# A four-layer graph network on one Trainium2 core: its layers on two scaled 16-bit floats a value, with the count matrix read in place

## The chip, the cores and the metric

The kernel runs on one core of one Trainium2 chip. The metric is the device time in microseconds (us), shown as the median of several executions. Everything is one launch.

## The reference

There are 2048 nodes with 512 features and 67,584 edges: 32,768 random pairs, their reverses and one loop a node, sorted by destination. Four blocks follow one another, each as x = x + block(relu(layernorm(x))):

```python
# block 0: attention inside each of 32 graphs of 64 nodes, 8 heads, a bias per edge added to the scores
attn = einsum(q, k) * scale; attn[b, src, dst] += edge_attr @ We + be; out = softmax(attn) @ v @ Wo + bo
# block 1: three GCN layers; deg counts the in-edges plus the loop, dis = rsqrt(deg)
h = segment_sum((h @ W)[row] * dis[row] * dis[col], col) + b        # relu after the first and the second
# block 2: one GCN layer with the degrees counted at the source, bias inside, relu outside
out = relu(segment_sum(dis[row] * dis[col] * (x @ W.T + b)[row], col))
# block 3: a sum with one weight an edge
out = relu(segment_sum((features @ W)[src' ] * edge_weight, dst'))
```

So five products (2048x512 by 512x512) are each followed by a sum over neighbours. The kernel does the sums of blocks 1 and 2 as products with a dense matrix of edge counts (2048x2048), and the last as a product with a dense matrix of summed edge weights.

## The kernel before, in words

It has four stages, one after another. **Edge prep** (`edge_prep`, to 68 us) counts edges, computes the edge biases, the degrees (`keep.dis1`, one reciprocal root a node) and the statistics of the first layer norm. **Build** (`build_matrices`, to about 497 us) takes the edges in 64 batches. In each, VectorE (DVE) makes one-hot matrices, TensorE (PE) multiplies them (L875 for the attention bias, L880 for counts and weights), ScalarE (ACT) copies counts and the first part of the weights out of PSUM, and DVE adds the second part into `w_slab` (L651). PE transposes the slab four batches later (L826), and it goes to DRAM as f32. The projections q, k and v are spread over the same batches (L853, L860). **Attention** ends at 665 us. The rest are the **layers** (`graph_layers`).

The engines are programmed one by one; each runs its own list in order and waits on semaphores. `keep.count` holds the counts as f16, `[partition, source tile, destination]`, with the destinations in an order of class (node within its graph) and then graph. A value of the layers is held as two fp32r parts: `hi` is the value cast (ACT), and `lo` is the value less `hi` (DVE).

- `products(layer)`: for each of 16 tiles, `split_hi` (ACT, L1430) and `split_lo` (DVE, L1669) write two parts of the transposed input, PE runs 12 matmuls of 512 columns (hi.hi, hi.lo, lo.hi over 4 blocks; L1573), and `product_hi` (ACT, L1445) and `product_lo` (DVE, L1682) put the scaled result into `m.g` as two parts. There are two PSUM banks for it. In the fourth layer DVE first adds the bias (L1676).
- `sums(layer)`, for the first four layers: four groups `c` of 512 destinations, 16 steps `i` in each, 8 matmuls a step (L1607) into four banks. Ahead of each step `copy_chunk` (DVE, L1692) rewrites 128x512 counts from f16 to fp32r in natural node order. At the end of a group DVE's `finish` reads the four banks (L1713 in layers 0 and 1), and PE's first step of the next group waits bank by bank for it. In layer 0, DVE also sums the count rows (`sum_out`, L1742), which the fourth layer's degrees need.
- The last layer's sum is 32 steps of 24 matmuls (L1645) on the f32 weight matrix. Each 128x1024 piece is split into parts by ACT (L1536) and DVE (L1767); the result is taken by DVE with relu and x added (L1794).

Layers are numbered 0 to 4 in the code. SyncE (SP) issues loads and stores in one fixed list. Weights share the buffer `m.tiles` with the tiles of x, or `h_t` for the first.

Of the kernel before, what the change touches and what calls it, by code (L numbers as in the profile page):

```python
# [22 lines left out]
NGRAPH = N // GN  # L23

# [17 lines left out]
LN_EPS = 1e-5  # L42

# [18 lines left out]
def prep_memory(nc, mem, keep, m):  # L62
# [24 lines left out]
    m.x_all = keep.count[:].rearrange("p t n -> p (t n)").bitcast(F32)[:, 0:NT * D].rearrange("p (t d) -> p t d", d=D)  # L87
# [21 lines left out]
    m.chosen = small[:, 9 * GN:10 * GN]  # L109
    m.graph_of = small[0:NGRAPH, 11 * GN:11 * GN + 2 * P].rearrange("p (z n) -> p z n", z=2)  # L110
# [4 lines left out]
             "most most_row most_one most_all mask graph_of starts_mm padded var std pool dve "  # L115
# [26 lines left out]
def prep_pool(nc, io, keep, m, s):  # L142
# [38 lines left out]
    pool.wait_ge(s["mask"], 1)  # L181
    for half in range(2):
# [15 lines left out]
def prep_act(nc, io, keep, m, s):  # L198
# [15 lines left out]
    act.sqrt(keep.dis1[:], keep.dis1[:])  # L214
    act.wait_ge(s["var"], 1)
# [3 lines left out]
def prep_pe(nc, io, keep, m, s):  # L219
# [74 lines left out]
    pe.matmul(m.most_ps, m.most_one.to_broadcast([2, P]), keep.ident[0:2, 0:2], start=True, stop=True).then_inc(s["most_all"], 1)  # L294


def prep_dve(nc, io, keep, m, s):
# [74 lines left out]
    op.then_inc(s["graph_of"], 1)  # L372
    dve.wait_ge(s["viol_row"], 1)
# [34 lines left out]
    dve.tensor_scalar(keep.dis1[:], m.deg_ps, 1.0, 1.0, ALU.add, ALU.max).then_inc(s["deg"], 1)  # L408
# [21 lines left out]
    dve.reciprocal(keep.dis1[:], keep.dis1[:])  # L430
    settle(dve.reciprocal(keep.rstd[:], keep.rstd[:]))
# [26 lines left out]
def build_memory(nc, mem, keep, m):  # L458
# [13 lines left out]
    m.w_slab = sb("w_slab", [P, 2, NT, P], F32)  # L472
# [93 lines left out]
def build_dve(nc, io, keep, m, s, first_round):  # L566
# [62 lines left out]
    def evacuate(n):  # L629
# [59 lines left out]
def build_act(nc, io, keep, m, s, first_round):  # L689
# [36 lines left out]
    def copy_sums(n):  # L726
# [72 lines left out]
def build_pe(nc, io, keep, m, s, first_round):  # L799
# [18 lines left out]
    def turn_weights(c):  # L818
# [339 lines left out]
def attention_dve(nc, io, keep, m, s, order):  # L1158
# [3 lines left out]
    for t in range(NT):  # L1162
        diag = keep.count[:, t].rearrange("p (v g) -> p g v", g=NGRAPH)[:, 2 * t:2 * t + 2]
# [57 lines left out]
    dve.tensor_scalar(keep.rstd[:], m.moments[:, :, 1], LN_EPS, None, ALU.add).then_inc(s["var"], 1)  # L1221
# [654 lines left out]
```

## Time and profile before

| | us |
|---|---|
| median of 3 runs | 1617.23 |
| lowest, highest | 1615.29, 1624.25 |
| the profiled execution's own time | 1615.48 |
| its span, first to last instruction | 1614.2 |
| PE busy | 1449.1 |
| DVE busy | 998.7 |
| ACT busy | 529.0 |
| mean granted PE clock, share of full speed | 0.958 |

"Busy" is the union of an engine's instructions. Matmuls are pipelined, so the time of one is longer than the pace at which they follow one another; the pace comes from a burst's length and count. The name `a<-b,c` of a matmul gives output, moving operand, stationary operand. `PEld` is PE's load of the stationary operand. Idle time in square brackets stands ahead of an instruction, with what ended it.

### The profile page before, as it was taken

The page shows a single profiled execution, that of the slowest core. Times are in us where ns is not written, and L with a number is a line of the kernel's source. Part 1 is how long each engine was busy: PE and PEld are TensorE (multiplying, and loading weights), DVE is VectorE, ACT ScalarE, POOL GpSimd, SP SyncE. Part 2 cuts the span into 40 slices and gives each one's busy share as a digit, 9 for nine tenths or more (in the row PEclk, how much of TensorE's full clock was granted, in tenths as well). Part 3 has the DMA queues.
Part 4 walks back from the last instruction along what each step waited for, and adds up shares of the span by engine and source line. Part 5 has one row for each costly group of instructions (what it writes and reads, how often), then busy time and mean ns, then how long its engine had stood idle before and what let it go on. Part 6 is the DMA issues. An engine that isn't in the chain of part 4 may idle for free.

```text
span 1614.2 us, 22068 instructions
## 1 busy us (share of the span) xinstructions
PE 1449.1 (90%) x8875; PEld 1183.5 (73%) x8875; DVE 998.7 (62%) x1487; ACT 529.0 (33%) x994; POOL 96.6 (6%) x74
## 2 busy tenths in 40 slices
PE   7389998999983778499999999999989999799999
PEld 6378887878772444378887888787867777678887
DVE  8789999899996665135884544455546544432322
ACT  1255666545542332462103210321124122432121
POOL 3010010101002300000000000011110000000000
PEclk9689999999996999799999999999999999899999
DMA  7423333344227332320000000002110221642301
GB/s 268 139 68 135 123 117 110 115 143 137 94 94 268 117 112 79 105 78 27 0 1 1 26 1 0 1 26 79 59 52 27 66 66 53 234 168 94 104 1 53
DMA packets 70111, 138.89 MB, mean 86 GB/s; under 512 B 9713, under 2 KB 22129, under 8 KB 68466
## 3 DMA queue, kind: packets, MB, share of 16 engines
q1 hardware_dynamic: 67362, 126.25, 22.5%
q0 software_dynamic: 1280, 5.77, 1.3%
q10 hardware_dynamic: 1360, 5.38, 0.9%
q8 instruction: 73, 1.20, 0.3%
q14 instruction: 36, 0.29, 0.1%
HBM read 84.06 MB, written 53.31 MB: 85 GB/s over the span
## 4 chain that ended last, share of the span: by engine, by line
PE 54%; DVE 2%; ACT 1%; DMA 1%; issue 1%; SPq 0%; DVEq 0%; ACTq 0%
PE banks L1607 29%; PE banks L1573 13%; PE banks L1645 11%; PE banks L1550 1%; DMA h_gcn_t<-in_L_gnn_W 0%; PE banks L1621 0%; DVE tiles L1721 0%; DVE split L1669 0%; DVE g L1682 0%; DMA b_row<-in_L_gnn_b 0%; ACT h_gcn_t L1497 0%; ACT g L1445 0%; DVE tiles L1794 0%; ACT h_gcn L1401 0%; ACT split L1430 0%
## 5 line engine op out<-in xcount | busy, mean ns | idle before, releaser
L1692 DVE CAST split<-count 128x512 fp32r<-128x512 f16 x256 | 162.8, 648 | 192.8 <-PE banks L1607 192.8
L1607 PE MATMUL banks<-g,split 128*128 128x512 f32 x1024 | 244.6, 395 | 0.7 <-DVE tiles L1721 0.6
L1573 PE MATMUL banks<-split 128*128 128x512 f32 x960 | 231.7, 401 | 12.9 <-DVE split L1669 12.6
L1607 PE MATMUL banks<-split,g 128*128 128x512 f32 x1024 | 233.9, 390 | 0.0
L1573 PEld LDWEIGHTS banks<-split 128*128 128x128 f32 x960 | 183.4, 193 | 56.9 <-DVE split L1669 18.5
L1607 PEld LDWEIGHTS banks<-split,g 128*128 128x128 f32 x1024 | 191.2, 188 | 42.4 <-DVE h_gcn_t L1713 3.2
L1607 PEld LDWEIGHTS banks<-g,split 128*128 128x128 f32 x1024 | 188.0, 188 | 45.9 <-DVE tiles L1717 2.8
L1645 PE MATMUL banks<-g,split 128*128 128x512 f32 x768 | 176.0, 392 | 2.9 <-DVE split L1767 2.9
L1645 PEld LDWEIGHTS banks<-g,split 128*128 128x128 f32 x768 | 145.2, 189 | 33.7 <-DVE split L1767 3.3
L627 DVE TENSOR_TENSOR x_sb<-eb_parts,x_sb 128x4096 f16<-128x4096 f16 x64 | 146.5, 2289 | 0.0
L875 PE MATMUL bias_ps<-x_sb 128*128 128x256 f16 x1024 | 125.0, 276 | 17.5 <-DVE bias L637 15.4
L875 PEld LDWEIGHTS bias_ps<-x_sb 128*128 128x128 f16 x1024 | 100.1, 99 | 41.8 <-DVE x_sb L627 16.4
L1767 DVE TENSOR_TENSOR split<-count,split 128x1024 fp32r<-128x1024 f32 x32 | 39.0, 1225 | 119.1 <-ACT split L1536 119.1
L1682 DVE SCALAR_TENSOR_TENSOR g<-banks,dis,g 128x512 fp32r<-128x512 f32 x64 | 48.0, 750 | 75.2 <-ACT g L1445 74.7
L1669 DVE TENSOR_TENSOR split<-h_gcn_t,split 128x512 fp32r<-128x512 f32 x80 | 54.7, 685 | 51.4 <-ACT split L1430 51.4
L1149 PE MATMUL wo_ps<-wo_sb,att_t 128*128 128x512 f32 x128 | 67.3, 674 | 19.9 <-ACT att_t L1082 19.9
L616 DVE TENSOR_TENSOR x_sb<-iota_src,keys 128x2048 f16<-128x2048 f16 x64 | 78.3, 1223 | 0.0
L1445 ACT ACTIVATE g<-banks,dis 128x512 fp32r<-128x512 f32 x64 | 44.1, 689 | 97.3 <-PE banks L1573 68.1
L1536 ACT CAST split<-count 128x1024 fp32r<-128x1024 f32 x32 | 33.3, 1048 | 129.8 <-PE banks L1645 129.8
L1497 ACT ACTIVATE h_gcn_t<-h_gcn_t,b_col 128x512 f32<-128x512 f32 x32 | 20.5, 712 | 161.2 <-DVE h_gcn_t L1713 161.2
L651 DVE SCALAR_TENSOR_TENSOR w_slab<-cw_ps,w_first 128x512 f32<-128x512 f32 x64 | 67.5, 1054 | 8.9 <-ACT w_first L737 8.8
L1430 ACT CAST split<-h_gcn_t 128x512 fp32r<-128x512 f32 x80 | 49.2, 617 | 47.5 <-PE banks L1607 47.5
(212 smaller groups left out, 1811.3 us busy)
## 6 DMA issues: line engine op xcount, KB each, us to landing
weight_dram<-w_new SPq DMA_DIRECT2D x64, 256.0 KB, 2.4
count<-weight_dram SPq DMA_DIRECT2D x32, 512.0 KB, 6.7
tiles<-x_dram SPq DMA_DIRECT2D x48, 256.0 KB, 2.6
qk_dram<-stage SPq DMA_DIRECT2D x64, 128.0 KB, 1.9
qk<-qk_dram SPq DMA_DIRECT2D x8, 1024.0 KB, 6.9
x_dram<-tiles SPq DMA_DIRECT2D x32, 256.0 KB, 2.2
count<-in_x SPq DMA_DIRECT2D x4, 1024.0 KB, 11.8
h<-in_x SPq DMA_DIRECT2D x16, 256.0 KB, 3.7
```

Of the source, the lines that this page charges most:

```text
L616: dve.tensor_tensor(m.hot_src[:, z].rearrange("p g (c two) -> p g c two", two=2), keep.iota_src[:].rearrange("p (c two) -> p c two", two=2 ...
L627: dve.tensor_tensor(m.hot_eb[:, z].rearrange("p g (t c) -> p g t c", t=NT), values, tiles, ALU.mult).then_inc(s["hots"], 1)
L651: dve.scalar_tensor_tensor(slab, m.cw_ps[:, :, 2 * CCOLS:CW].rearrange("p b (h s) -> p b h s", h=2), 1.0 / LOW, m.w_first[:].rearrange("p ...
L875: mm = pe.matmul(m.bias_ps[:, 0:NT * HP], m.hot_src[:, z, g], m.hot_eb[:, z, g], start=g == 0, stop=g == BATCH - 1)
L1149: mm = pe.matmul(m.wo_ps[:, t % 2], m.att_t[:, k, :], m.wo[:, k, :], start=k == 0, stop=k == KT - 1)
L1430: act.copy(m.h_parts[:, t % 2, 0], m.h_t[:, :, t * P:(t + 1) * P]).then_inc(s["hi"], 1)
L1573: mm = pe.matmul(m.prod_ps[:, slot], m.h_parts[:, slot, zh, k], m.w_parts[:, zw, k], start=n == 0, stop=n == len(passes) - 1)
L1607: mm = pe.matmul(m.agg_ps[:, b], lhs, rhs, start=i == 0 and z == 0, stop=i == NT - 1 and z == 1)
L1645: mm = pe.matmul(m.banks[:, b], m.part[:, n % 3, z, b * P:(b + 1) * P], m.g[:, q, gz], start=q == 0 and (z, gz) == (0, 0), stop=q == NT - ...
L1669: dve.tensor_tensor(m.h_parts[:, t % 2, 1], m.h_t[:, :, t * P:(t + 1) * P], m.h_parts[:, t % 2, 0].bitcast(F32), ALU.subtract).then_inc(s[ ...
L1682: dve.scalar_tensor_tensor(lo, result, dis[:, t:t + 1], hi.bitcast(F32), ALU.mult, ALU.subtract).then_inc(s["glo"], 1)
L1692: dve.tensor_copy(m.chunk[:, n % 4].rearrange("p (g v) -> p g v", v=GN), keep.count[:, i].rearrange("p (v g) -> p g v", g=NGRAPH)[:, graph ...
```

## The change

- Everything in the layers that was fp32r becomes f16 in two parts, with power-of-two scales. Each weight matrix, each group of 512 columns of h in layers 1 and 2, and the edge weights get a scale from their largest absolute value. The maximum is reduced along the free dimension on DVE, moved to one row by a PE transpose (`peak_row`), turned into an exponent in a row of small DVE operations on one partition, and sent to all partitions by a small matmul (`peak_all`).
- The counts are f16 operands in place: `copy_chunk`, `m.chunk` and its 256 copies go. `keep.count` is now `[P, NT, GROUPS, GN, GPC]`, that is by chunk of 512 destinations, class and the 8 graphs of the chunk. So the sums come out in that order: `finish` of layers 0 and 1 writes back to natural order, x is loaded and stored in that order by DMA (`x_own`), the fourth layer's split reads `h_t` through a strided view, and a second set of degrees (`odis1`, `odis2`) is made in that order, with new work in edge prep and in layer 1.
- `w_slab` is written in the order of the sums, and the PE transposes read it with a stride.
- `sum_out` takes a maximum of each count row besides the sum, and all 16 tiles are done at four a group, ahead of `finish`.
- Layers 1 and 2 use three PSUM banks for products, and `product_hi`/`product_lo` run one tile later. Weights have a buffer of their own; three pieces of the edge weights are loaded early; relu after the last sum moves from DVE to ACT.

```diff
-    m.g = sb("g", [P, NT, 2, D], F32R)
-    m.split = sb("split", [P, 3, KT * D], F32R)
+    m.g = sb("g", [P, NT, 2, D], F16)
+    m.h_parts = sb("h_parts", [P, 2, 2, KT, P], F16)
+    m.w_parts = sb("w_parts2", [P, 2, KT, D], F16)
+    m.part = sb("part", [P, 3, 2, HALF], F16)
...
-        slab = m.w_slab[:, q % 2].rearrange("p s (c b h) -> p c b h s", c=4, h=2)[:, n % 4]
-        dve.scalar_tensor_tensor(slab, m.cw_ps[:, :, 2 * CCOLS:CW].rearrange("p b (h s) -> p b h s", h=2), 1.0 / LOW,
-                                 m.w_first[:].rearrange("p b (h s) -> p b h s", h=2), ALU.mult, ALU.add).then_inc(s["slab"], 1)
+        slab = m.w_slab[:, q % 2, n % 4].rearrange("p (b c) -> p b c", b=BATCH)
+        dve.scalar_tensor_tensor(slab, m.cw_ps[:, :, 2 * CCOLS:CW], 1.0 / LOW, m.w_first[:], ALU.mult, ALU.add).then_inc(s["slab"], 1)
...
+        tiles = m.w_slab[:, q % 2].rearrange("p c (u s) -> p s (c u)", s=NT)
...
# PE, sums
-            pe.wait_ge(s["chunk"], layer * STEPS + n + 1)
-                        lhs, rhs = m.g[:, i, z, block], m.chunk[:, n % 4]
+                            lhs, rhs = m.g[:, i, z, block], m.count[:, i, c]
...
+                if c == 0:
+                    if i == 2:
+                        pe.wait_ge(s["glo"], (layer + 1) * NT)
+                        peak_row()
+                    if i == 4:
+                        peak_all()
...
+                elif layer < 2:
+                    if i == 6:
+                        peak_row()
+                    if i == 8:
+                        peak_all()
...
# PE, products
+            if layer in (1, 2) and t == 2:
+                peak_row()
+            if layer in (1, 2) and t == 3:
+                peak_all()
...
# DVE
+    def exponent():
+        dve.wait_ge(s["peak_row"], peaks + 1)
+        settle(dve.tensor_reduce(m.line[:, 8:9], m.peak_row, axis=AX.X, op=ALU.max))
+        settle(dve.tensor_scalar(m.line_i[:, 0:1], m.line[:, 8:9].bitcast(I32), 23, None, ALU.logical_shift_right))
+        settle(dve.tensor_scalar(m.line_i[:, 0:1], m.line_i[:, 0:1], 16, None, ALU.max))
...
+    def h_scale(layer, c):
+        row = m.h_line[:, layer - 1]
+        for k in range(KT):
+            dve.wait_ge(s["relu_h"], ((layer - 1) * GROUPS + c) * KT + k + 1)
+            op = dve.tensor_reduce(m.h_max[:, k:k + 1], m.h_t[:, k, c * COLS:(c + 1) * COLS], axis=AX.X, op=ALU.max)
+        settle(op)
+        dve.tensor_reduce(m.peak[:, 0:1], m.h_max[:], axis=AX.X, op=ALU.max).then_inc(s["peak"], 1)
+        exponent()
...
+            to_all(op, m.h_scale[:, layer - 1, c:c + 1], 1).then_inc(s["h_scaled"], 1)
...
# DVE, finish of layers 0 and 1
-                dve.tensor_tensor(m.h_t[:, b, cols], m.agg_ps[:, b], m.dis_row[:, cols], ALU.mult).then_inc(s["fin"], 1)
+                out = m.h_t[:, b, c * COLS:(c + 1) * COLS].rearrange("p (g v) -> p v g", g=GPC)
+                pair = [a.rearrange("p (v g) -> p v g", g=GPC) for a in (m.agg_ps[:, b], m.dis_row[:, c * COLS:(c + 1) * COLS])]
+                dve.tensor_tensor(out, *pair, ALU.mult).then_inc(s["fin"], 1)
...
+            if c == GROUPS - 1:
+                split_lo(layer + 1, 2)
+            h_scale(layer + 1, c)
...
     def sum_out(i):
-        dve.tensor_reduce(m.dis2[:, i:i + 1], keep.count[:, i], axis=AX.X, op=ALU.add).then_inc(s["out_sum"], 1)
+        row = m.count[:, i].rearrange("p c n -> p (c n)")
+        dve.tensor_reduce(m.dis2[:, i:i + 1], row, axis=AX.X, op=ALU.add)
+        dve.tensor_reduce(m.count_max[:, i:i + 1], row, axis=AX.X, op=ALU.max).then_inc(s["out_sum"], 1)
...
# DVE, sums
+        for c in range(GROUPS):
+            if c == 0:
+                weight_peak(layer + 1)
+                weight_scale(layer + 1)
+                if layer == 1:
+                    edge_scale()
+                    out_degrees()
+                for k in range(KT):
+                    weight_lo(layer + 1, k)
...
+            if layer == 0:
+                for i in range(PER):
+                    sum_out(c * PER + i)
...
+            finish(layer, c)
...
# the split of the fourth layer reads h_t so
+        cols = m.h_t[:].rearrange("p k (c v g) -> p k c g v", c=GROUPS, g=GPC)[:, :, t // PER, first:first + 2]
```

## Rows read from the trace of the kernel before

**Rows 1.** The page, part 1: busy time by engine over the span.

```profile
PE 1449.1 (90%) x8875; PEld 1183.5 (73%) x8875; DVE 998.7 (62%) x1487; ACT 529.0 (33%) x994; POOL 96.6 (6%) x74
```

**Rows 2.** The chain that ended last, by line (the page, part 4, second line).

```profile
PE banks L1607 29%; PE banks L1573 13%; PE banks L1645 11%; PE banks L1550 1%; DMA h_gcn_t<-in_L_gnn_W 0%; PE banks L1621 0%; DVE tiles L1721 0%; DVE split L1669 0%; DVE g L1682 0%; DMA b_row<-in_L_gnn_b 0%; ACT h_gcn_t L1497 0%; ACT g L1445 0%; DVE tiles L1794 0%; ACT h_gcn L1401 0%; ACT split L1430 0%
```

**Rows 3.** Busy time in stretches: us, PE, PEld, DVE, ACT, POOL, PE clock, DMA.

```profile
200.00:300.00 100.00, 93.47 (x780) 82.01 (x779) 93.51 (x122) 59.05 (x111) 9.59 (x4) 0.98 0.35 118
...
sum 405.00, PE 373.45 PEld 328.21 DVE 382.98 ACT 222.49 POOL 32.74; mean PE 62.24 PEld 54.70 DVE 63.83 ACT 37.08 POOL 5.46
...
740.00:857.00 117.00, 117.00 (x515) 95.75 (x514) 84.03 (x98) 11.29 (x19) 0.00 (x0) 1.00 0.03 10
...
1246.00:1372.00 126.00, 125.27 (x565) 99.98 (x563) 61.29 (x118) 30.07 (x83) 0.00 (x0) 1.00 0.19 59
```

**Rows 4.** The chain in order of time, pieces of the layers.

```profile
665.81 8.03 DMA h_gcn_t<-in_L_gnn_W
...
678.78 4.67 PE banks L1621 x32
...
740.30 116.83 PE banks L1607 x512
...
864.12 38.37 PE banks L1573 x168
...
1434.86 171.23 PE banks L1645 x747
```

**Rows 5.** Engines in order of time, build: start, us, engine, line, count.

```profile
301.13 1.91 PE L875 MATMUL bias_ps<-x_sb 128*128 128x256 f16 x16
...
303.56 0.62 PE L826 MATMUL work_ps<-ident,w_slab 128*128 128x128 f32 x4
...
208.67 1.14 PE L815 MATMUL work_ps<-ident,gathered 128*128 128x128 f32 x8
```

**Rows 6.** Groups of instructions by line and form, 120 to 560 us.

```profile
L651 DVE SCALAR_TENSOR_TENSOR w_slab<-cw_ps,w_first 128x512 f32<-128x512 f32 x59 | 62.2, 1054 | 7.1 <-ACT w_first L737 6.9
...
L595 DVE SCALAR_TENSOR_TENSOR fields<-fields,scale,eb_parts 128x1024 f32<-128x1024 f32 x7 | 14.5, 2068 | 0.0
...
L716 ACT ACTIVATE eb_parts<-fields 128x1024 f16<-128x1024 f32 x7 | 13.8, 1973 | 0.0
```

**Rows 7.** The same view, 665 to 1614 us.

```profile
L1767 DVE TENSOR_TENSOR split<-count,split 128x1024 fp32r<-128x1024 f32 x32 | 39.0, 1225 | 119.1 <-ACT split L1536 119.1
...
L1536 ACT CAST split<-count 128x1024 fp32r<-128x1024 f32 x32 | 33.3, 1048 | 129.8 <-PE banks L1645 129.8
...
L1742 DVE TENSOR_REDUCE dis<-count 128x1 f32<-128x2048 f16 x16 | 36.5, 2279 | 0.0
...
L1713 DVE TENSOR_TENSOR h_gcn_t<-banks,dis_row 128x512 f32<-128x512 f32 x32 | 19.8, 678 | 0.0
...
L1669 DVE TENSOR_TENSOR split<-h_gcn_t,split 128x512 fp32r<-128x512 f32 x80 | 54.7, 685 | 51.4 <-ACT split L1430 51.4
...
L1692 DVE CAST split<-count 128x512 fp32r<-128x512 f16 x256 | 162.8, 648 | 192.8 <-PE banks L1607 192.8
```

**Rows 8.** Engines in order of time, at three idle stretches of PE.

```profile
864.12 16.16 PE L1573 MATMUL banks<-split 128*128 128x512 f32 x70 [1.56 <-DVE split L1669]
...
1200.97 5.49 PE L1573 MATMUL banks<-split 128*128 128x512 f32 x12 [5.64 <-DVE split L1669]
...
1434.86 7.34 PE L1645 MATMUL banks<-g,split 128*128 128x512 f32 x24 [2.88 <-DVE split L1767]
```

**Rows 9.** The chain in order of time, products of the fourth layer.

```profile
1238.27 0.71 DVE banks L1676
...
1241.13 3.07 PE banks L1573 x12
```

**Rows 10.** Engines in order of time, two dependent small operations on DVE.

```profile
66.58 0.17 DVE L423 TENSOR_SCALAR small_i<-small 128x2 int32<-128x2 int32 x1
66.78 0.17 DVE L424 TENSOR_SCALAR small_i<-small_i 128x2 int32<-128x2 int32 x1
```

More of the change, by code:

```diff
@@ L1319, in layers_sp @@
         load_x(t, t % PER)
-    sp.wait_ge(s["relued"], NT)
-    load_weights(1)
-    for layer in (2, 3):
+    for n in range(AHEAD):
+        load_raw(n)
+    for layer in (1, 2, 3):
         sp.wait_ge(s["wlo"], KT * layer)
@@ L1438, in product_hi @@
             act.wait_ge(s["agg"], NT * layer)
-        if layer == 4:
-            act.copy(m.g[:, t, 0], m.prod_ps[:, t % 2]).then_inc(s["ghi"], 1)
-        else:
-            dis = m.dis2 if layer == 3 else keep.dis1
-            if layer == 3:
-                act.wait_ge(s["dis2"], 1)
-            act.activation(m.g[:, t, 0], m.prod_ps[:, t % 2], ACT.Copy, scale=dis[:, t:t + 1]).then_inc(s["ghi"], 1)
+        if layer < 3:
+            act.wait_ge(s["g_scaled"], layer + 1)
+        if layer == 3:
+            act.wait_ge(s["odis2"], 1)
+        scale = G_SHIFT[4] if layer == 4 else m.g_scale[:, layer, t:t + 1]
+        act.activation(m.g[:, t, 0], prod_bank(m, layer, t), ACT.Copy, scale=scale).then_inc(s["ghi"], 1)
     def products(layer):
-        for t in range(NT + 1):
+        late = slots(layer) - 1
+        for t in range(NT + late):
             if t < NT:
@@ L1560, in turn_weights, with peak_row, peak_all @@
         for i in range(KT):
-            mm = pe.transpose(m.turn_ps[:, bank, i * P:(i + 1) * P], m.tiles[:, o, i * P:(i + 1) * P], keep.ident[:])
+            mm = pe.transpose(m.turn_ps[:, bank, i * P:(i + 1) * P], m.w_raw[:, o, i * P:(i + 1) * P], keep.ident[:])
         mm.then_inc(s["wturned"], 1)
+    def peak_row():
+        pe.wait_ge(s["peak"], peaks + 1)
+        pe.transpose(m.peak_row, m.peak[:, 0:1], keep.ident[:]).then_inc(s["peak_row"], 1)
+    def peak_all():
+        nonlocal peaks
+        peaks += 1
+        pe.wait_ge(s["peak_one"], peaks)
+        pe.matmul(m.peak_all, m.ones[:], m.line[:, 0:8], start=True, stop=True).then_inc(s["peak_all"], 1)
     def product(layer, t):
@@ L1616, in layers_pe, with turn_own @@
+    def turn_own():
+        pe.wait_ge(s["dis2_t"], 1)
+        for c in range(GROUPS):
+            for z in range(2):
+                mm = pe.matmul(m.own_ps[:, c], m.spread[:, z, c], m.dis2_t[:, z * GN:(z + 1) * GN], start=z == 0, stop=z == 1)
+        mm.then_inc(s["own"], 1)
     turn(0, 0)
     turn(0, 1)
+    peak_row()
+    peak_all()
     for c in range(GROUPS):
@@ L1695, in products @@
+        dve.scalar_tensor_tensor(lo, result, scale, hi, ALU.mult, ALU.subtract).then_inc(s["glo"], 1)
     def products(layer):
[L1696 to L1697 removed]
+        late = slots(layer) - 1
+        for t in range(NT + late):
+            if t < NT and (t >= (3 if layer in (1, 2) else 2) or layer in (0, 4)):
                 split_lo(layer, t)
[L1699 to L1703 removed]
+            if t >= late:
+                product_lo(layer, t - late)
@@ L1768, in layers_dve @@
+    weight_peak(0)
+    weight_scale(0)
     for k in range(KT):
```

524 lines of the change are left out of this document (329 added, 195 removed).

## The prediction

> **What bounds the kernel now.** I read the page first: PE is busy 90% of the span, DVE 62% [rows 1]. Then the chain that ended last, by line: L1607 (sums), L1573 (products) and L1645 (last sum) hold 53% of the span, all PE [rows 2]. In the table of stretches the layers' sums have PE full (117.00 of 117) at clock 1.00, while the build has both PE and DVE above 90% [rows 3]. So the layers are PE's own pace, and the build is a race of two engines. The pace: 512 matmuls in 116.83 us, 168 in 38.37, 747 in 171.23 are 228.2, 228.4 and 229.2 ns [rows 4].
>
> **Matmuls on f16.** Their number stays: 960 products, 2048 in sums, 768 in the last sum. 512 columns of f16 don't occur before. 256 do, each with another stationary operand: 16 in 1.91 us [rows 5]. With the last one's drawn-out end taken off (about 0.28), the pace is 109 ns, 2.3 above 256 columns at 2.4 GHz; 512 columns then take 213.3 + 2.3 = 215.7 ns. Ends: 228.2 (nothing gained) and 213.3. I take 215.7, the nearest row's. That is 12.5 ns a matmul: 512 give 6.4 us, a warm layer of products at most 2.2, and 768 at 229.2 give 10.3.
> The Trainium skill ("TensorE: Matmul & The Clock Gate", Back-to-back issue gap) also states about 131 ns a matmul for a sustained stream of 512 columns with loads. It would take some 320 us more off (3776 x 85 ns). This trace is against it: 109 ns for half the columns. I give it 1%.
>
> **Strides.** Three rows show what strided f32 work costs. L651 writes with a 512 B step and takes 1054 ns where the contiguous L1713 takes 678: 0.72 ns an element. L595 reads one f16 operand at 32 B steps: 2068 against 1225 for L1767, 0.8 an element. L716 (ACT) reads at 512 B steps: 1973 against 1048 for L1536, 0.9 [rows 6, 7]. Against this stands L1692, a plain copy reading f16 at 64 B steps in 648 ns [rows 7]. The change removes one such access and adds others:
> - Slab: L651 falls to about 0.69, so 64 x 0.36 = 23 us of DVE. But PE is busy 373 of the 405 us from 92 to 497, DVE 383 [rows 3]. With DVE at 361 PE leads, and both hand over through single buffers. The gain lies between 6 and 23; I take 14. The slab's strided loads by PE: eight transposes with strided loads take 1.14 us, four contiguous 0.62 [rows 5], so 121 ns against 114, under 2 us in all, within the 14.
> - `finish` in layers 0 and 1 writes at 256 B steps: 1.04 us a bank for 0.68. PE takes a bank's first two matmuls in 0.43, so each group boundary waits some 1.4 us more.
> - The fourth layer's split reads at 32 B steps on ACT (+0.45) and DVE (+0.4).
>
> The Trainium skill ("SBUF — State Buffer", Door 1: The DMA port swizzle) says that accesses landing on a new 16-byte line each pay. L651, L595 and L716 agree, L1692 doesn't. By the rule the two new strided places cost as above; without it they cost nothing.
>
> **Layer 0's sums: DVE becomes the bound.** `sum_out` is now two reductions of 2048 f16 for each of 16 tiles. One takes 2279 ns (2.19 apart) [rows 7]; a group has 8 = 17.5 us, before its `finish`. A group of PE is 128 x 0.2157 = 27.6 us. In the first group DVE does the last `product_lo` (1.5), the weight maximum (2048 f32, 2.2), waits for PE's small matmuls after steps 2 and 4 (to 9.2), splits weights (to 12.2), and sums (to 29.7). The four banks are free at 33.7, and PE's first step of group 1 ends at 34.2 instead of 29.6. Call the end of that step E. Now `h_scale` of the group before stands in DVE's list ahead of the next sums. It waits for `peak_row` after PE's step 6 (E+10.4) and `peak_all` after step 8 (E+13.8), so it ends at E+14.3. Then 17.5 and four banks at about 1 us: E+36.2, where PE alone needs 27.6. PE idles 6.6 us in between. That happens twice, and the third time DVE reaches layer 1's first `split_lo` at E+31.8+0.7.
> After 5.64 us of idle, PE ran 12 matmuls in 5.49 us, after 2.88 us 24 in 7.34, after 1.56 at full pace [rows 8]: 2.7, 1.8 and 0 us extra at the lower clock. Adding 2.7 twice and 1.8 once: 34.2 + 36.2 + 38.9 + 38.9 - 3.7 + 1.8 = 146.3 us until layer 1's first product, against 116.8: **+29.5**. Ends: below, if reductions were hidden, -5 (6.4 less inserted PE work); above, 40 with slower rewarming.
>
> **Change of layer, 0 to 1 and 1 to 2.** Product 3 of the next layer now needs `g_scale`, and this the maximum over group 3: four banks (4.0), relu on ACT, `split_lo(2)` (0.7), four reductions (2.4), `peak_row`, some ten dependent small operations at 0.2 each [rows 10], `peak_all`, then ghi, glo, split (2.2). PE covers it with products 0 to 2 (7.8) and stands still 2.3 + 2.9 us; before, it was 1.56 [rows 8]. Cost 3.4 us plus 2.6 of lower clock: **+6.0** for 1 to 2. For 0 to 1 DVE starts late, and I count **+7.2**. Ends: 0 and 10 each.
>
> **The other terms** (- is a gain):
> - Edge prep: six more DVE operations (0.2 to 0.5 each) in DVE's filled list before the barrier: +1.9. POOL's three new ones lie under its wait for the edge records.
> - Start of layers: first weights are waited for 8.03 us [rows 4]; now they are issued first, but the maximum and exponent (4.5) follow. ACT meanwhile waits for PE's 4.67 us of `dis` rows [rows 4] as before: +1.
> - Products: layer 0 -1 (ACT is nearly full there), 1 and 2 -2 each.
> - Sums of layer 1: -6.4; boundaries +1.4 x 3; `out_degrees` waits for PE's steps 11 and 13, so weights and `finish` are late by 1.2; inserted PE work 2.2: +1.2. Layers 2 and 3: -6.2 and -6.1. The 256 copies L1692 (163 us of DVE) were hidden behind PE and give nothing.
> - Products of layer 3: before, two products ran per 2.86 (end of one to start of the next but one, 1238.27 to 1241.13) + 3.09 [rows 9], 2.97 each. Now 2.86 + 0.84 + 2.94, 3.32 each; 14 of them +4.9. The missing bias load gives 0.4: +4.5. Without stride costs -1.4.
> - Into layer 4: the first piece of edge weights is split ahead of it (+1.7), one copy instead of four (-0.3): +1.4. Products -2.2; the wait of 2.88 before the last sum [rows 8] goes: -2.8. Last sum -10.3. Relu on ACT at the end +0.7.
>
> **Sum**: 1.9 - 14 + 1 - 1 + 29.5 + 7.2 - 2 + 1.2 + 6.0 - 2 - 6.2 + 4.5 - 6.1 + 1.4 - 2.2 - 2.8 - 10.3 + 0.7 = +6.8. On the profiled execution's 1615.5: 1622.3. The median of the runs stands 1.7 above that execution, so **1624 us**.
>
> **Rivals.**
> 1. Strides are free and the build gives 20. Then -6 (layer 3), -11 (eight `finish`), -6 (build): **1601**. For it: L1692. Against: three rows. 0.26.
> 2. Layer 0's sums stay PE-bound, since the reductions run faster than the row: 29 less, **1595**. Against: the maximum is the same operation on the same data, and the list is in order. 0.06.
> 3. Slower: the lower clock after each new stop. I count six stops. If the many short waits (each bank of `finish`, about 1 us) keep PE from the upper level for 24 to 40 matmuls instead of 12, each of six costs 3 to 6 more: **1642**, and it decides from about 20 matmuls on. For it: 24 matmuls were slowed after only 2.88 us [rows 8]. 0.17.
> 4. f16 is no faster than fp32r, because the 15 ns above 213.3 aren't the type's: +47, **1670**. Against: the f16 row. 0.05.
> 5. The 131 ns rule, 0.01.
> The forecast has 0.45; its own range is 1612 to 1636.
>
> About 0.5% (8 us) can be told from no change. Faster: rivals 1, 2, 5: 0.33. The forecast's 0.45 splits into 0.26 same and 0.19 slower; with rivals 3 and 4 slower is 0.41. The range 1597 to 1648 takes in rival 1 and 3.
>
> **What would show it.** The sums' matmuls at 215 to 216 ns; slab writes near 0.69 us; idle PE of 5 to 7 us ahead of groups 2 and 3 of layer 0, released by DVE's `finish`, with 32 reductions of 2.28; two idles of 2 to 3 us at each change of layer; 1.04 us for `finish`; 3.3 us a product in layer 3. It is wrong if layer 0's sums end within 125 us, or if the matmul's pace stays at 228.

## The result, and the profile after

Four runs of the changed kernel have their median at 1629.33 us (1627.98 to 1631.36), four of the kernel before (the three of the table and one more) at 1618.06 (1615.29 to 1624.25): a ratio of 1.0065, 95% interval [1.0034, 1.0097]. The change costs 11 us by the medians; I forecast 1624. The profiled execution took 1629.89 us, its span is 1628.2.

The page, part 1, answers to [rows 1]: PE's busy time fell by 12 us although the span grew by 14.

```profile
PE 1437.2 (88%) x8942; PEld 859.9 (53%) x8942; DVE 933.9 (57%) x1449; ACT 557.0 (34%) x963; POOL 86.3 (5%) x79
```

The chain of waits of the changed kernel, in order of time (start, us, what), answers to [rows 4].

```profile
662.45 5.79 DMA tiles<-x_dram
...
764.60 15.24 PE banks L1718 x56
...
802.44 15.10 PE banks L1718 x56
...
840.15 15.02 PE banks L1718 x56
...
892.91 35.53 PE banks L1681 x156
...
1056.85 4.28 PE banks L1681 x12
...
1099.64 5.18 PE banks L1718 x24
...
1459.76 160.12 PE banks L1784 x741
```

24 matmuls in 5.18 us are 215.8 ns each, 741 in 160.12 are 216.1, where [rows 4] had 228 to 229. But layer 0's sums, one piece of 116.83 us before, are now cut up by stops, stretches in which PE stands idle (the number in brackets, in us):

```profile
764.60 1.93 PE L1718 MATMUL banks<-count,g 128*128 128x512 f16 x4 [3.24 <-DVE h_gcn_t L1926]
...
802.44 1.03 PE L1718 MATMUL banks<-count,g 128*128 128x512 f16 x2 [6.53 <-DVE h_gcn_t L1926]
...
840.15 15.02 PE L1718 MATMUL banks<-count,g 128*128 128x512 f16 x56 [6.54 <-DVE h_gcn_t L1926]
```

After each stop 56 matmuls take 15.0 to 15.2 us (269 ns) instead of 12.1. The granted clock behind it is 0.50, the lower level of 1.2 GHz (columns: us, PE, PE clock, DMA share and GB/s):

```profile
764.60:770.00 5.40, 5.40 (x13) 0.50 0.00 0
```

The stretch of layer 0's sums (columns as in [rows 3]), where before PE was busy 117.00 of 117 us at clock 1.00:

```profile
733.20:877.50 144.30, 121.73 (x526) 51.31 (x523) 99.82 (x104) 14.22 (x19) 0.00 (x0) 0.93 0.02 8
```

VectorE in order of time in the second group of those sums (start, us, engine, line, what, count, idle time before and who ended it):

```profile
763.53 3.68 DVE L1926 TENSOR_TENSOR h_gcn_t<-banks,dis_row 128x512 f32<-128x512 f32 x4
767.06 2.44 DVE L1861 TENSOR_REDUCE h_max<-h_gcn_t 128x1 f32<-128x512 f32 x4
769.53 0.16 DVE L1863 TENSOR_REDUCE peak<-h_max 128x1 f32<-128x4 f32 x1
779.99 0.28 DVE L1806 TENSOR_REDUCE line<-banks 1x1 f32<-1x128 f32 x1 [10.30 <-PE banks L1661]
...
783.75 0.16 DVE L1823 COPY h_scale<-banks 128x1 f32<-128x1 f32 x1 [2.41 <-PE banks L1668]
783.83 2.27 DVE L1955 TENSOR_REDUCE dis<-count 128x1 f32<-128x2048 f16 x1
...
799.18 2.27 DVE L1956 TENSOR_REDUCE count_max<-count 128x1 f32<-128x2048 f16 x1
801.37 3.69 DVE L1926 TENSOR_TENSOR h_gcn_t<-banks,dis_row 128x512 f32<-128x512 f32 x4
```

From one `finish` to the next are 37.8 us, where PE needs 27.6. VectorE stands still for 10.3 + 2.4 us of them, waiting for PE's small matmuls of `peak_row` and `peak_all`, while eight reductions of the counts are queued behind that wait. Then PE, done with its group, stands still for VectorE: the 6.53 us ahead of 802.44, and 6.54 us ahead of 840.15. Each engine waits once for the other.

The groups of instructions answer to [rows 6, 7] (line, engine, what, count | busy us, mean ns | idle before; L685 in the build, L1926 in the layers, L1496 in the products of layer 3 alone):

```profile
L685 DVE SCALAR_TENSOR_TENSOR w_slab<-cw_ps,w_first 128x512 f32<-128x512 f32 x64 | 43.6, 681 | 14.5 <-ACT w_first L770 14.1
...
L1926 DVE TENSOR_TENSOR h_gcn_t<-banks,dis_row 128x512 f32<-128x512 f32 x32 | 29.7, 1044 | 30.9 <-PE banks L1718 30.9
...
L1496 ACT CAST h_parts<-h_gcn_t 128x512 f16<-128x512 f32 x20 | 20.2, 1015 | 0.0
```

The span, cut at events that both traces have. Each length is read between two starts, each trace being one execution; the starts of matmuls that overlap can be read 0.2 us apart, so tenths are not to be leaned on. The forecast's terms are grouped to the same cuts.

| stretch | before | after | forecast | measured |
|---|---|---|---|---|
| edge prep | 67.9 | 72.4 | +1.9 | +4.5 |
| build and attention | 596.4 | 589.0 | -14 | -7.4 |
| into the layers | 24.7 | 23.6 | +1 | -1.1 |
| products, layer 0 | 51.2 | 48.2 | -1 | -3.0 |
| sums, layer 0 | 116.9 | 144.3 | +29.5 | +27.4 |
| change and products, layer 1 | 45.3 | 50.9 | +5.2 | +5.6 |
| sums, layer 1 | 116.9 | 120.6 | +1.2 | +3.8 |
| change and products, layer 2 | 45.1 | 50.6 | +4.0 | +5.5 |
| sums, layer 2 | 125.6 | 119.3 | -6.2 | -6.2 |
| change and products, layer 3 | 57.0 | 61.3 | +4.5 | +4.2 |
| sums, layer 3 | 123.6 | 118.0 | -6.1 | -5.6 |
| into layer 4 | 15.1 | 16.2 | +1.4 | +1.1 |
| products and last sum | 220.3 | 205.4 | -15.3 | -14.9 |
| end | 8.1 | 8.3 | +0.7 | +0.2 |
| sum | 1614.2 | 1628.2 | +6.8 | +14.0 |

### The profile page after: what moved, and what is told of

Same layout as the page of the kernel before. It is cut to its first block, busy times and chain, and to the rows that moved or that the text cites. A ratio compares the mean times of both kernels' runs of the same rounds, so it can differ in the third digit from the quotient of the medians.

```text
span 1628.2 us, 22078 instructions
## 1 busy us (share of the span) xinstructions
PE 1437.2 (88%) x8942; PEld 859.9 (53%) x8942; DVE 933.9 (57%) x1449; ACT 557.0 (34%) x963; POOL 86.3 (5%) x79
## 4 chain that ended last, share of the span: by engine, by line
PE 47%; DVE 8%; ACT 2%; issue 1%; DMA 0%; ACTq 0%; DVEq 0%; SPq 0%
PE banks L1718 24%; PE banks L1681 11%; PE banks L1784 10%; DVE dis L1955 2%; DVE count_max L1956 2%; PE banks L1644 1%; DVE h_parts L1897 1%; DVE h_gcn_t L1926 1%; ACT h_parts L1496 1%; DVE banks L1905 1%; ACT h_gcn L1465 0%; PE banks L1760 0%; DMA tiles<-x_dram 0%; DVE tiles L1930 0%; DVE stats L1942 0%
## 5 line engine op out<-in xcount | busy, mean ns | idle before, releaser
L1681 PE MATMUL banks<-w_parts,h_parts 128*128 128x512 f16 x960 | 225.5, 396 | 31.5 <-DVE h_parts L1897 19.8
L1718 PE MATMUL banks<-count,g 128*128 128x512 f16 x1024 | 235.0, 389 | 20.0 <-DVE h_gcn_t L1926 20.0
L1718 PE MATMUL banks<-g,count 128*128 128x512 f16 x1024 | 229.5, 379 | 1.1 <-DVE tiles L1934 0.9
L1681 PEld LDWEIGHTS banks<-w_parts,h_parts 128*128 128x128 f16 x960 | 95.2, 101 | 156.5 <-DVE h_parts L1897 26.8
L1718 PEld LDWEIGHTS banks<-count,g 128*128 128x128 f16 x1024 | 98.6, 99 | 149.4 <-DVE h_gcn_t L1926 33.9
L1784 PE MATMUL banks<-g,part 128*128 128x512 f16 x768 | 166.1, 379 | 0.1
L1718 PEld LDWEIGHTS banks<-g,count 128*128 128x128 f16 x1024 | 98.5, 98 | 119.6 <-DVE tiles L1934 6.7
L1784 PEld LDWEIGHTS banks<-g,part 128*128 128x128 f16 x768 | 75.1, 98 | 91.0 <-DVE g L1908 0.6
L1908 DVE SCALAR_TENSOR_TENSOR g<-banks,g_scale,g 128x512 f16<-128x512 f32 x64 | 47.9, 748 | 37.8 <-ACT g L1510 37.8
L894 PE MATMUL work_ps<-h_t,wq_sb 128*128 128x256 f32 x256 | 60.3, 384 | 0.0
L894 PE MATMUL work_ps<-h_t,wk_sb 128*128 128x256 f32 x256 | 59.4, 380 | 0.2 <-ACT fields L734 0.2
```

What stands on the lines that cost most here:

```text
L894: mm = pe.matmul(m.work_ps[:, bank, 0:SCOLS], weights[:, k, c * P:(c + 1) * P], m.h_t[:, k, :], start=k == 0, stop=k == KT - 1)
L1681: mm = pe.matmul(prod_bank(m, layer, t), m.h_parts[:, slot, zh, k], m.w_parts[:, zw, k], start=n == 0, stop=n == len(passes) - 1)
L1718: mm = pe.matmul(m.agg_ps[:, b], lhs, rhs, start=i == 0 and z == 0, stop=i == NT - 1 and z == 1)
L1784: mm = pe.matmul(m.banks[:, b], m.part[:, n % 3, z, b * P:(b + 1) * P], m.g[:, q, gz], start=q == 0 and (z, gz) == (0, 0), stop=q == NT - ...
L1908: dve.scalar_tensor_tensor(lo, result, scale, hi, ALU.mult, ALU.subtract).then_inc(s["glo"], 1)
```

## The experiments

The ratios below are to the kernel before, measured beside each run, with a 95% interval. The changed kernel stands at 1.0065 [1.0034, 1.0097], so its time can't be told from a run whose ratio lies within some 0.3% of it. There the profile of the stage decides, and that is one execution. Differences from the changed kernel in us are between medians taken at different times.

**1. The slab alone, on the kernel before.**

```diff
-        slab = m.w_slab[:, q % 2].rearrange("p s (c b h) -> p c b h s", c=4, h=2)[:, n % 4]
...
+        slab = m.w_slab[:, q % 2, n % 4].rearrange("p (b c) -> p b c", b=BATCH)
...
+        tiles = m.w_slab[:, q % 2].rearrange("p c (u s) -> p s (c u)", s=NT)
```

> The kernel before with one part of the change: the slab is written in the order of its sums, and the transposes read it with a step. The stage from the start of the build to the last slab write took 420.5 us before and 413.3 in the changed kernel, with PE busy 93 and 96% of it. Theory A (PE is what the build waits for once the slab write costs 0.68 instead of 1.05 us): the stage takes 412 to 415 us, the kernel is 6 to 8 us faster than before, and PE is busy over 95% of the stage. Theory B (the changed kernel lost part of the slab's gain to its four smaller count additions, or to other memory places): the slab alone gives the 14 us of the forecast or more, the stage takes 407 or less. Theory C (the slab gives nothing, the stage differs by chance): within 1 us of before.

1608.7 us, 0.9933 [0.9907, 0.9959]. From the end of edge prep to the start of the last slab write are 415.3 us: 5.2 less than before, 0.3 above theory A's upper end; B and C are out. The changed kernel has 413.3, so its smaller count additions cost nothing that this stage shows.

**2. The same without the step in the transposes' reads.** The weight matrix comes out in a wrong order, so this run serves for its times alone.

```diff
-        tiles = m.w_slab[:, q % 2].rearrange("p c (u s) -> p s (c u)", s=NT)
+        tiles = m.w_slab[:, q % 2].rearrange("p c (u s) -> p (c u s)", s=NT).rearrange("p (s u) -> p s u", s=NT)
```

> As the run before it, but the transposes read 128 neighbouring elements of the slab instead of every 16th, so the weight matrix comes out in a wrong order; every instruction is there. Strided weight loads took 196 ns in the changed kernel against 141 contiguous ones before. Theory A (PE binds, and the strided loads are part of what PE does): PE's busy time falls by about 3 to 4 us (256 transposes by some 0.014 us, 64 groups), the stage takes 409 to 411 us, 10 us below before. Theory D (the loads are hidden, PE's hand-over with VectorE through single buffers binds): within 1 us of the run with the step.

1608.4 us, 0.9947 [0.9926, 0.9968]: the times don't tell it from run 1. The stage takes 412.4 us, 2.9 less, in one profile each; eight profiles with the changed kernel's build, steps and all, have 411.1 to 413.5, so a difference of this size is near the spread. The transposes themselves are clearer. Their loads (duration ns min/median/max), and the transposes in PE (busy us, mean ns), with the step (run 1):

```profile
L826 PEld LDWEIGHTS work_ps<-ident,w_slab x256: 186/196/210, 115.8 to 487.3; 128*128 128x128 f32 x128
...
L826 PE MATMUL work_ps<-ident,w_slab 128*128 128x128 f32 x256 | 42.9, 292 | 1.5 <-DVE w_slab L651 1.5
```

and without it (run 2):

```profile
L826 PEld LDWEIGHTS work_ps<-ident,w_slab x256: 138/141/145, 116.9 to 485.1; 128*128 128x128 f32 x128
...
L826 PE MATMUL work_ps<-ident,w_slab 128*128 128x128 f32 x256 | 39.3, 278 | 1.5 <-DVE w_slab L651 1.5
```

Busy times from 92 to 484 us, of the kernel before, of run 1 and of run 2:

```profile
sum 392.00, PE 368.34 PEld 323.85 DVE 380.20 ACT 217.81 POOL 32.74; mean PE 92.09 PEld 80.96 DVE 95.05 ACT 54.45 POOL 8.19
```

```profile
sum 392.00, PE 378.26 PEld 333.92 DVE 366.79 ACT 219.07 POOL 28.57; mean PE 94.57 PEld 83.48 DVE 91.70 ACT 54.77 POOL 7.14
```

```profile
sum 392.00, PE 373.95 PEld 329.94 DVE 368.09 ACT 220.25 POOL 28.69; mean PE 93.49 PEld 82.48 DVE 92.02 ACT 55.06 POOL 7.17
```

VectorE was the fuller engine before. With its slab writes cut by 24 us PE is the fuller one (96%), and without the step PE is busy for 4.3 us less, 3.6 of them in the transposes. So the build gains only until PE is in its way. The strided loads cost PE 3.6 us of work; that about 3 of them reach the stage fits the two profiles, but isn't shown by them alone. The Trainium skill ("SBUF — State Buffer", Door 1: The DMA port swizzle) has accesses that land on a new 16-byte line each pay; the loads with a 64 B step agree, 196 against 141 ns.

**3. The maxima of the counts away from layer 0.** The 16 reductions go to layer 1's groups, the edge scale to layer 2's.

```diff
-        dve.tensor_reduce(m.dis2[:, i:i + 1], row, axis=AX.X, op=ALU.add)
-        dve.tensor_reduce(m.count_max[:, i:i + 1], row, axis=AX.X, op=ALU.max).then_inc(s["out_sum"], 1)
+        dve.tensor_reduce(m.dis2[:, i:i + 1], row, axis=AX.X, op=ALU.add).then_inc(s["out_sum"], 1)
...
+            if layer == 1:
+                for i in range(PER):
+                    max_count(c * PER + i)
```

> The changed kernel with the 16 maximum reductions of the counts moved from layer 0's sums to layer 1's (4 in each group, behind the weights), and the edge scale that needs them to layer 2's. Nothing is left out. Per group VectorE then reduces 9.1 us instead of 18.2 in layer 0 and 9.1 instead of 0 in layer 1. Theory A (in layer 0 VectorE's list is the bound, because the reductions stand behind a scale that waits for PE's steps 6 and 8): the group's list ends at E+14.3+9.1 = E+23.4, before PE's 27.6, so layer 0's sums fall from 144.3 to 117 to 119 us, layer 1's stay at 120.6, the kernel takes 1602 to 1606 us. Theory B (the strided finish and the inserted PE work cost layer 0 its time, the reductions only happen to stand there): layer 0's sums stay above 130 us. Theory C (the work only moves the loss): layer 1's sums grow by over 10 us.

1606.2 us, 0.9944 [0.9921, 0.9966]. Layer 0's sums take 116.7 us. The two stretches of the sums in this run, layer 1's and layer 0's (columns as in [rows 3]), and the stop in layer 1's:

```profile
896.40:1026.00 129.60, 117.95 (x542) 52.30 (x541) 69.11 (x97) 14.33 (x20) 4.95 (x4) 0.96 0.06 17
729.50:846.20 116.70, 114.11 (x525) 50.27 (x524) 66.83 (x90) 14.22 (x19) 0.00 (x0) 1.00 0.03 10
...
936.59 3.76 PE L1718 MATMUL banks<-count,g 128*128 128x512 f16 x8 [9.92 <-DVE h_gcn_t L1926]
```

A is shown for layer 0: 27.6 us came from one list. The strided `finish` and the inserted PE work are still there, so B is out. C was half right: layer 1's sums grew by 9.0, since in its first group the reductions stand behind `out_degrees`, which waits for PE's steps 11 and 13, and VectorE reached `finish` only at 935.5. The net gain of the two stretches is 18.6 us. Of the 24 us by which this profile is shorter than the changed kernel's, 3.6 lie ahead of the layers, where the edit touches nothing.

**4. Fixed factors for layers 1 and 2's values.** In place of the measured ones; the groups' reductions, exponents and PE's small matmuls for them are left out.

```diff
-            op = dve.tensor_reduce(m.h_max[:, k:k + 1], m.h_t[:, k, c * COLS:(c + 1) * COLS], axis=AX.X, op=ALU.max)
...
-        exponent()
...
+        if c < GROUPS - 1:
+            dve.memset(m.h_scale[:, layer - 1, c:c + 1], 2.0 ** 12).then_inc(s["h_scaled"], 1)
```

> The changed kernel with fixed factors (2^12) for layers 1 and 2's values instead of measured ones: the eight groups' reductions, the exponents on one partition and PE's two small matmuls for each are left out. Both count reductions stay in layer 0. Theory A (layer 0 loses its time to VectorE's wait for PE's steps 6 and 8 plus the 18.2 us of reductions, and the two changes of layer lose 5 us each to the chain from the last bank to g_scale): with the wait gone a group's list ends at about E+4.3+18.2 = E+22.5, before 27.6, so layer 0's sums fall to 117 to 119 us (-26), the stretches from the end of the sums to the next layer's sums fall from 50.9 and 50.6 to about 45 (-5.5 each), 1591 to 1595 us in all. Theory B (volume of the reductions alone is the bound): layer 0's sums stay above 130. Theory C (the changes of layer lose to the strided finish and the split, not to the scale): they stay at 49 to 51.

1585.1 us, 0.9799 [0.9773, 0.9825]. Layer 0's sums take 120.2 us with all 32 count reductions in place, so volume alone (theory B) is out: either cure works, because the loss needs the wait and the reductions behind it. What is left above run 3 is the first stop, still 3.23 us: in the first group the reductions stand behind the weight's scale, which waits for PE's steps 2 and 4. The changes of layer are read in the chain of this run:

```profile
853.65 41.44 PE banks L1681 x192
895.09 5.18 PE banks L1714 x24
...
1014.28 41.44 PE banks L1681 x192
```

16 products without any stop are 41.4 us, for 50.9 and 50.6 in the changed kernel, so theory C is out. I had expected 45: that was the stretch before, which held its own stop and the slower matmuls. The scale costs 9.5 and 9.2 us, not 5.5.

**5. The fourth layer's reordering on ScalarE's copies.**

```diff
+            out = m.h_t[:].rearrange("p k (c g b v) -> p k c b v g", c=GROUPS, g=GPC, b=PER)[:, :, c, b]
+            for k in range(KT):
+                op = act.copy(out[:, k], source[:, k].rearrange("p (v g) -> p v g", g=GPC))
...
-        cols = m.h_t[:].rearrange("p k (c v g) -> p k c g v", c=GROUPS, g=GPC)[:, :, t // PER, first:first + 2]
```

> The changed kernel with the reordering for the fourth layer done where ScalarE copies the transposed tiles out of PSUM (it writes them in the natural order, four copies of 128x128 instead of one of 128x512), so that the two splits of that layer read neighbouring elements. Nothing is left out. Before it, one product of that layer takes 3.45 us, a chain through two engines: bias addition 0.70, g's high half 0.69, split 1.11 on ScalarE with a step, split 1.07 on VectorE with a step. Theory A (this chain sets the layer, and the step costs what the forecast took, 0.4 to 0.45 on each engine): the period falls to 2.6 to 2.75, where PE takes over, and the products' stretch from 61.3 to about 50 us, -10 us in all (1619). Theory B (the layer is bound elsewhere, the split's step only fills idle time): no more than 2 us. Theory C (the strided write costs ScalarE what the strided reads did, and the last chunk's four copies lie in the chain): -5 us.

1620.4 us, 1.0028 [1.0010, 1.0047]: 9 us below the changed kernel by the medians, 6 by the ratios. The groups of instructions from 720 to 1400 us:

```profile
L1478 ACT COPY h_gcn_t<-banks 128x128 f32<-128x128 f32 x64 | 16.7, 414 | 30.9 <-PE banks L1646 30.9
L1502 ACT CAST h_parts<-h_gcn_t 128x512 f16<-128x512 f32 x20 | 12.2, 615 | 0.0
```

ScalarE's split fell from 1015 to 615 ns, VectorE's from 1.07 to 0.68 us, the period of the layer's last products from 3.45 to 2.83 (two in 5.66, from 1260.56 to 1266.22) and the stretch from 61.3 to 52.5. The products before them are slower in both kernels (two in 6.69 from 1238.11 here, in 8.07 from 1240.19 in the changed kernel). A is shown, though PE didn't take over: 2.83 is above its 2.59. The copies grew from 585 to 4 x 414 ns, but beside PE's sums.

**6. `finish` without a step, relu with one.**

```diff
-                out = m.h_t[:, b, c * COLS:(c + 1) * COLS].rearrange("p (g v) -> p v g", g=GPC)
...
-                dve.tensor_tensor(out, *pair, ALU.mult).then_inc(s["fin"], 1)
+                if layer * GROUPS + c:
+                    dve.wait_ge(s["relu_h"], (layer * GROUPS + c - 1) * KT + b + 1)
+                dve.tensor_tensor(m.own_order[:, b], m.agg_ps[:, b], m.dis_row[:, c * COLS:(c + 1) * COLS], ALU.mult).then_inc(s["fin"], 1)
...
-                act.activation(part, part, ACT.Relu, bias=m.b_col[:, layer, k:k + 1],
+                act.activation(part.rearrange("p (g v) -> p v g", g=GPC), m.own_order[:, k].rearrange("p (v g) -> p v g", g=GPC), ACT.Relu, bias=m.b_col[:, layer, k:k + 1],
```

> The changed kernel with the reordering of the first two layers' results moved from VectorE to ScalarE: VectorE multiplies into another buffer in the order of the sums (no step), ScalarE's relu, which follows anyway, writes it into natural order. Nothing is left out. Theory A (PE waits at each group's boundary for four banks at 1.04 us, of which 0.36 is the step): a boundary costs PE 4 x 0.36 = 1.4 us less, in layer 1 three times and once at the end of each layer, in layer 0 the same in VectorE's list: -9 to -11 us in all if ScalarE writes with the step at no cost, 1 us less gain if each relu grows by 0.3 us (the last group's lies in the chain to g_scale). Layer 1's sums fall from 120.6 to 116 to 117. Theory B (the step costs VectorE nothing that anybody waits for): within 2 us.

1623.1 us, 1.0033 [1.0020, 1.0046]: 6 us below the changed kernel by the medians, 5 by the ratios.

```profile
L1565 ACT ACTIVATE h_gcn_t<-part,b_col,unscale 128x512 f32<-128x512 f32 x32 | 35.1, 1243 | 206.6 <-DVE part L1927 206.6
...
L1927 DVE TENSOR_TENSOR part<-banks,dis_row 128x512 f32<-128x512 f32 x32 | 19.8, 681 | 30.9 <-PE banks L1719 30.9
```

`finish` costs 681 ns for 1044, and layer 1's sums take 116.9 us for 120.6: 1.2 a boundary. Layer 0's sums gain 3.3. But the relus went from 814 to 1243 ns, and the last group's four lie in the chain to g_scale, so the changes of layer gained nothing (50.8 each).

**7. Edge prep without the second set of degrees.**

```diff
-    for c in range(GROUPS):
-        mm = pe.matmul(m.own_ps[:, c], m.spread[:, c], m.cnt, start=True, stop=True)
...
-    settle(dve.tensor_tensor(m.own[:], m.own_ps, keep.own_mask[:].unsqueeze(1).to_broadcast([P, GROUPS, GN]), ALU.mult))
-    settle(dve.tensor_reduce(keep.odis1[:], m.own[:].rearrange("p c (b v) -> p (c b) v", b=PER), axis=AX.X, op=ALU.add))
```

> The changed kernel without the degrees in the order of the sums: the first stage's spread copy, its four small matmuls, the multiplication and the reduction are left out (the degrees by tile are used in their place). The stage ended at 72.2 to 72.3 us in three profiles of kernels with it and at 67.7, 69.1 and 70.0 in three without. Theory A (these operations on VectorE's filled list are the stage's whole growth, 2 us by the forecast, 3.3 by those means): it ends at 69 to 70.5 us and the kernel is 2 to 3.3 us faster. Theory B (something else in the stage grew, as POOL's work or the order of transfers): it ends at 72.

1627.7 us, 1.0062 [1.0039, 1.0085]: by time alone not told from the changed kernel. (The profiled execution, 1621.1, is the lowest of its four.) The stage's last operation:

```profile
69.13 0.17 DVE L457 SCALAR_TENSOR_TENSOR shift<-stats,rstd 128x16 f32<-128x16 f32 x1
```

It starts at 67.72, 69.14, 69.99 and 69.13 in the four profiles without these operations (before, runs 1, 2 and 7) and between 71.61 and 72.40 in the seven with them. So they cost 3.1 us by the means, theory A; the profile of before was 1.3 below its kind. A part of it is this wait of VectorE for PE in the changed kernel, which run 7 doesn't have:

```profile
51.53 0.34 DVE L414 TENSOR_TENSOR_SCAN small<-small,misc_ps 32x64 f32<-32x64 f32 x1 [1.03 <-PE misc_ps L302]
```

**8. Runs 3, 5 and 6 together,** with the maxima in the third layer's groups 1 to 3 and the edge scale in the fourth layer's.

```diff
+            if layer == 2 and c:
+                for i in range((0, 0, 6, 11)[c], (0, 6, 11, 16)[c]):
+                    max_count(i)
```

> The changed kernel with the reorderings of the two runs above, and the counts' maximum reductions in the third layer's groups 1 to 3 (6, 5 and 5), the edge scale in the fourth layer's. Nothing is left out. With the reductions moved to layer 1 the time was 24 us lower, of which layer 0's sums gave 28 and layer 1's first group took 7 back. Theory A (the parts add, layer 2 has room for the reductions): 1629 - 28 - 10 - 10 = 1578 to 1584 us, about 2% below before. Theory B (layer 2's groups have no room either, with their statistics behind the reductions): 7 us more, 1588.

1582.8 us, 0.9779 [0.9760, 0.9797]. The parts add: layer 0's sums take 113.0 us, layer 1's 116.4, and the change and products of layer 3 take 52.8, as in run 5. Layer 2's sums stay at 119.2: it had room.

**9. VectorE's order at a change of layer, on top of run 8.**

```diff
-            if c == GROUPS - 1:
-                split_lo(layer + 1, 2)
             h_scale(layer + 1, c)
...
         dve.tensor_reduce(m.peak[:, 0:1], m.h_max[:], axis=AX.X, op=ALU.max).then_inc(s["peak"], 1)
+        if c == GROUPS - 1:
+            split_lo(layer, 2)
         exponent()
```

> The run before this one (both reorderings moved, maxima in the third layer) with VectorE's order at the end of layers 0 and 1 changed: the four maximum reductions of the last group come before the low half of the next layer's third tile, not behind it. Nothing is left out. There VectorE stood idle 3.25 us for ScalarE's high half of that tile, then 0.75 us of split, then 2.46 us of reductions, and PE waited 2.67 us for the maximum and 2.72 us before the fourth product. Theory A (the chain from the last bank to g_scale sets the change of layer, and VectorE's order is in it): the reductions run beside ScalarE's relus, the maximum is there about 3 us sooner, PE doesn't wait before the third product, and the fourth starts 2.5 us sooner: twice, -5 us, 1578 us. Theory B (the chain is bound by ScalarE's relus with their step, 1.25 us each, and PE's first three products): no more than 1 us each, 1581 or more.

1575.6 us, 0.9754 [0.9728, 0.9780]: faster than before by 2.5%, and than the changed kernel by 54 us. PE at the change from layer 1 to 2, run 8:

```profile
1016.93 0.27 PE L1664 MATMUL banks<-ident,peak 128*1 128x128 f32 x1 [2.67 <-DVE peak L1866]
1017.04 2.75 PE L1684 MATMUL banks<-w_parts,h_parts 128*128 128x512 f16 x12
...
1022.82 3.44 PE L1684 MATMUL banks<-w_parts,h_parts 128*128 128x512 f16 x9 [2.72 <-DVE h_parts L1898]
```

and run 9:

```profile
1008.27 0.27 PE L1664 MATMUL banks<-ident,peak 128*1 128x128 f32 x1
1008.85 2.76 PE L1684 MATMUL banks<-w_parts,h_parts 128*128 128x512 f16 x12 [0.31 <-DVE h_parts L1900]
...
1014.64 7.69 PE L1684 MATMUL banks<-w_parts,h_parts 128*128 128x512 f16 x27 [2.71 <-DVE h_parts L1900]
```

The first wait went from 2.67 to 0.31 us, the second stayed. From the start of layer 0's sums to that of layer 1's are 158.3 us for 163.6, and 163.5 for 165.5 to layer 2's. The first gained more than its stop. Behind it the chain of run 8, and the stretch after it (same columns), have

```profile
855.80 36.75 PE banks L1684 x156
...
856.00:860.00 4.00, 4.00 (x10) 0.50 0.02 4
```

and those of run 9

```profile
852.87 33.84 PE banks L1684 x156
...
853.00:857.00 4.00, 4.00 (x20) 1.00 0.02 4
```

which is 236 against 217 ns a matmul: in run 8 PE came back at the lower clock, in run 9 at the full one. Theory A holds, with 7 us where I expected 5; 2.9 of the 7 are the clock at one place, which my expectation didn't have.

## Why the prediction held, and where its terms were off

The forecast case came true: the time is 5 above it and inside its own range, and the three large terms (matmuls, layer 0's sums, stops at the changes of layer) are what the traces show. The build's term was twice too large, and part of the agreement is luck: the sum was 7.2 short of the two profiles, and the medians lie only 5 apart because the profiled execution of before was 2.6 below the median of its four.

- **Matmuls on f16** (12.5 ns each): right. 215.8 to 216.1 ns where I said 215.7, taken from rows with half the columns. The last sum with its products gave 14.9 of 15.3 us, layers 2 and 3's sums 11.8 of 12.3. Rivals 4 and 5 fell by this. PE's weight loads shrank as well (188 to 98 ns a load in the sums), and no run tells the type of the moving operand from that of the loaded one as the source of the 12.5 ns. The Trainium skill ("TensorE: Matmul & The Clock Gate", Back-to-back issue gap) has 131 ns for a sustained stream of 512 columns with loads; 741 at 216.1 ns are against it.
- **Layer 0's sums** (+29.5, +27.4): right in mechanism and size. Reductions of 2275 ns, stops of 3.2, 6.5, 6.5 and 6.3 us, and 3.0 us lost to the lower clock after each of the three inside the sums (56 matmuls in 15.1 for 12.1) where I took 2.7. Runs 3 and 4 show it from two sides. Rival 2 fell.
- **Slab** (-14, -7.4): the mis-sized term. "The gain lies between 6 and 23; I take 14" had the bound in it, PE leads, but no sum for its 6, nor for the 14 between the two. The slab alone gave 5.2 (run 1), as PE was busy 92% of the stretch already [rows 3]. The price of strided loads was too low as well. I took 121 against 114 ns a transpose, "under 2 us in all", from two bursts of different lines; the load takes 55 ns more, the transpose 14, which is 3.6 us of PE in all (runs 1 and 2).
- **What the single profiles leave open:** from the last slab write to the first product of layer 0 are 199.2 to 199.3 us in the changed kernel and runs 4 to 6, and 195.7 to 196.2 in runs 3, 7, 8 and 9, with the same code in that part. The difference lies in the attention stage and no run explains it. So "build and attention" could have read -11 as well as -7, and up to 3 us of the distance between the changed kernel and run 9 may not be the edits'.
- **Edge prep** (+1.9, +4.5): 3.1 of it is the change (run 7). I had counted the operations, not that VectorE would also wait for PE's matmuls there (1.03 us at 51.53). 1.3 is the draw of one profile.
- **Change of layer** (+5.2 and +4.0, +5.6 and +5.5): the two stops came as foretold, 2.2 and 2.7 us at the second. The third product ran at the lower clock there (12 matmuls in 4.44 us; granted clock 0.55 from 1058 to 1061), as counted. What I missed is that the loss could be seen against 41.4 us, not against the stretch before: run 4.
- **Sums of layer 1** (+1.2, +3.8): its boundaries cost what I said (run 6 took 3.7 back), the first group more.
- **Strides** (rival 1): fell by runs 5 and 6, in which the instructions without the step took 615 for 1015 ns and 681 for 1044, and the kernel 9 and 6 us less.
- **Two slips of arithmetic** in the prediction change nothing: 2.3 + 2.9 us of stops less the 1.56 of before are 3.6, not 3.4, and L651 against L1713 is 0.73 ns an element, not 0.72.
- **Rival 3** (a slow return of the clock at many short waits): stood at no place; the 3.0 us after a stop are 14 matmuls at twice 216 ns, not 24 to 40, and layer 1's boundaries lost what VectorE's banks explain.
- **Into the layers, and products of layer 0** (+1 and -1, -1.1 and -3.0): two small gains more than counted, which no run took apart.

The misses add up to 7.2: 6.6 in the build, 2.6 in edge prep, and the rest -2, in which layer 1's sums (+2.6) and the change to layer 2 (+1.5) are covered by gains elsewhere.

## What to carry to other kernels

Where an engine's list holds a wait for another engine's step in mid-group, all that is queued behind it is late by the whole wait: move work of no urgency (the maxima) to a stage in which the list idles. When two engines are both nearly full, relief of one is worth something only until the other leads: here 24 us less on VectorE gave 5 to 7, so take the lower end. The reordering had to be paid once, as an access with a step: let the engine pay that has idle time beside it (run 5), and keep it out of the chain that ends last (run 6 didn't, at the changes of layer).

## What the runs showed of the hardware that was not expected

- A weight load of 128x128 f32 whose elements lie 64 B apart took 196 ns (186 to 210, run 1), a contiguous one 141 (run 2).
- ScalarE writing 128x512 f32 in SBUF with a 256 B step took 1243 ns (run 6) for 814 without (the changed kernel), +0.84 ns an element, about what the step cost VectorE (1044 for 681, +0.71).
- After 2.19 us of idle time PE ran 12 matmuls at 370 ns each in one place, after 2.67 us 12 at 229 in another (1056.69 of the changed kernel, 1017.04 of run 8). In runs 8 and 9 the same stop of 2.72 us at the first change of layer was followed by a granted clock of 0.50 and of 1.00. It had another stop of 2.66 us 12 matmuls ahead of it in run 8 and one of 0.29 in run 9; but at the second change, with 0.31 ahead of 2.71, run 9's clock was 0.52 (1014.64 to 1018). The length of the idle time alone doesn't say whether the clock falls; what else does was not tried.
